# First expert stage of a four-layer kernel: three of sixteen token tiles dense instead of four, the first sorted group one tile larger, and several steps of VectorE, TensorE and GpSimd in other places

## The chip, the core and the metric

The program runs on one core of a Trainium2 chip. Its engines take instructions from queues of their own: TensorE (PE; its weight loads are listed as PEld), VectorE (DVE), ScalarE (ACT), GpSimd (POOL) and SyncE (SP), which here issues nearly all plain DMAs. They meet in semaphores only. The order of each engine's instructions is the order in which the program is written. The metric is the device time of one execution, in microseconds (us), as a median of runs.

## What is computed

Four layers with residual sums run over `x`, 4 batches x 512 positions x 128 features (2048 tokens of D = 128):

```python
x = x + ssm(layernorm(x), ...)          # linear recurrence over time, then W_out
x = x + ffn(layernorm(x), ...)          # first expert stage
x = x + attention(layernorm(x), ...)    # 16 heads of 64, relative bias, softmax
x = x + ffn(layernorm(x), ...)          # second expert stage, same weights

def ffn(x, router_w, w_gate, w_up, w_down):      # 8 experts, hidden 256
    xt = x.reshape(-1, D)
    logits = xt @ router_w.T
    topk_vals, topk_idx = jax.lax.top_k(logits, 2)
    g = jax.nn.sigmoid(topk_vals)
    g = g / (g.sum(axis=-1, keepdims=True) + 1e-10)
    out = jnp.zeros_like(xt)
    for e in range(8):
        ge = jnp.sum(jnp.where(topk_idx == e, g, 0), axis=-1)
        h = jax.nn.silu(xt @ w_gate[e]) * (xt @ w_up[e])
        out = out + ge[:, None] * (h @ w_down[e])
    return out.reshape(B, S, D)
```

Each token needs two of eight experts. Which two is known only when the logits of the layer are there.

## The kernel before

**Tiling.** The 2048 tokens are 16 tiles of 128, in four chunks of four tiles (QT = 4). `x_res` holds all of x on the chip. A product in fp32 precision is made of three products in a faster format (`three`, L301): high x high, high x low, low x high. So each operand exists as a rounded high part, made by ScalarE, and as a low part, the difference, made by VectorE or GpSimd.

**Two ways through an expert stage.** *Dense*: a set of tiles goes through all eight experts and the gates, zero where an expert was not chosen, weigh the sums. For expert e TensorE computes gates and up parts (`dense_gate_up`, 12 products with all tokens of the set as columns), ScalarE the silu, VectorE the product (`dense_products`), TensorE the tile sums (`dense_down`), and VectorE adds them to x with the gates as factors (`dense_add`). Nothing has to be sorted for it. *Sorted*: the tokens of a group of tiles are ordered by expert. VectorE works out the places (the `group_*` functions), GpSimd sends each tile's normalised rows to its two places in memory, one indirect DMA each (`scatter_rows`), SyncE loads the sorted rows back when all sends of the group have landed (`load_sorted`: blocks 0 to 3 as one transfer, the rest as another), and TensorE then takes them in blocks of 128 rows of one expert. A turn of sorted rows (`sorted_turn`) makes columns of rows, for up to four blocks at a time; such a piece has one bank for its outputs, a copy that empties it (`quad_out`), and one store to memory. For each block there follow three products of 512 columns (L303 to L305), the silu, the product, a turn, a copy and the down product (`block_down`). GpSimd gathers each tile's two rows back (`gather_rows`), and VectorE adds them to x with their gates (`combine`).

**The first expert stage before.** Chunk 0 (tiles 0 to 3) is dense. Group 0 is tiles 4 to 7: 8 sends, 15 blocks, in pieces of 4, 4, 4, 3. Group 1 is tiles 8 to 15: 16 sends, 23 blocks, in pieces of 4 five times, then 3. In all 38 blocks (`B1`). While the dense part runs, the norm of chunk 1 (`ln_*` with 1) and then the places of groups 0 and 1 are worked out on VectorE. GpSimd first makes low parts of weights: four experts, the query and key weights (L2079, 1024 columns each), the value weights (L2088), the other four experts. Then it sends, the sends of group 0 spaced over experts 4 to 7 and those of group 1 over expert 7 and the first blocks, one each time a step of TensorE is done. The norm that attention needs of chunk 0 is made in blocks 3 to 12 of the sorted part, right behind the dense sums, and its turn (`ln_turn`) stands on TensorE at block 11. The rows of group 0 come back from block 21 on and are added at blocks 31 and 32. Behind block 37 attention's first projections start (`enter`).

**The second expert stage** uses the same blocks in three groups: 2 (tiles 0 to 7, 23 blocks), 3 and 4 (four tiles, 15 blocks each). Group 4 is the last one; its routing is done between blocks of group 3, VectorE's and TensorE's parts in a hand-written order by steps of one block: the weights of group 3 at step 9, the sum and the maxima of group 4 at 11, its mask at 13, the gate weights of group 4 (`group_weights`) at 14, and at 15 the count (`group_count`, TensorE) and the places (`group_start`, VectorE). All waits are on constants.

## Time and profile before

| | |
|---|---|
| median of three runs (734.63, 734.91, 731.36) | 734.63 us |
| the profiled execution, its own time | 732.48 us |
| its span in the trace | 730.7 us |
| mean granted TensorE clock | 0.99 |
| TensorE busy | 688.5 us, 94% |
| VectorE busy | 550.6 us, 75% |
| ScalarE busy | 452.9 us, 62% |
| GpSimd busy | 306.4 us, 42% |
| chain that ended last | PE 77%, DVE 14%, ACT 4%, issue 3% |

Times within the program are counted from the start of the span. The dense part begins at about 49.7, the first block of the sorted part at 96.4, attention's first projection at 156.3. A row of a timeline gives the start, the duration of what stands in the row (of all of it, where it says x4 or so), the engine, the line and the operation, output first; in square brackets stands idle time of the engine ahead of it and what ended it. A row with x16 of an engine that works without a pause gives the cost of one as an average. A busy TensorE row can still be a slow one: the granted clock of a stretch is in the windows.

### The profile page before, as it was taken

The numbers are of one execution on the slowest core, as the hardware profiler recorded it, in microseconds if no ns is written. First come the engines' busy times: TensorE is split into PE (matmuls) and PEld (weight loads), VectorE is DVE, ScalarE is ACT, GpSimd is POOL, SyncE is SP. The second block draws the span as 40 slices with busy tenths as digits, with TensorE's granted clock in tenths as the row PEclk, the third lists the DMA queues.
The fourth block names the chain that finished last, engine by engine and source line by source line (L and its number), as shares of the span: only waits on it lengthen the run. The fifth ranks groups of instructions, "written<-read, shape, count | busy, mean of one in ns | idle before, by whom it ended". The sixth has DMA issues, their size and how long they took to land.

```text
span 730.7 us, 14144 instructions
## 1 busy us (share of the span) xinstructions
PE 688.5 (94%) x4316; PEld 485.0 (66%) x4316; DVE 550.6 (75%) x1712; ACT 452.9 (62%) x1097; POOL 306.4 (42%) x391
## 2 busy tenths in 40 slices
PE   4898998997899999998999999999999899998998
PEld 2576887885565755665666666576666566677886
DVE  7898774568998768877767769666988788476486
ACT  5546244556677757666757767667666768454554
POOL 1053471406674434333433333324365676503561
PEclk9999999999999999999999999999999999999999
DMA  9900054228000000000000000070003222032532
GB/s 236 290 5 0 30 202 137 71 68 304 19 23 4 3 0 1 2 1 1 1 1 1 2 1 1 1 190 3 1 9 105 73 69 62 23 92 66 133 84 59
DMA packets 52375, 43.37 MB, mean 59 GB/s; under 512 B 3296, under 2 KB 46944, under 8 KB 52304
## 3 DMA queue, kind: packets, MB, share of 16 engines
q1 hardware_dynamic: 48976, 35.63, 16.8%
q0 software_dynamic: 3328, 6.83, 3.2%
q8 instruction: 39, 0.64, 0.4%
q14 instruction: 32, 0.26, 0.1%
HBM read 26.70 MB, written 15.75 MB: 58 GB/s over the span
## 4 chain that ended last, share of the span: by engine, by line
PE 77%; DVE 14%; ACT 4%; issue 3%; POOL 0%; DMA 0%; DVEq 0%; ACTq 0%; POOLq 0%
PE psum L1166 15%; PE psum L1148 12%; PE psum L1133 12%; PE psum L303 8%; PE psum L305 6%; PE psum L304 6%; PE psum L816 5%; PE psum L1090 4%; DVE prob L1329 3%; PE psum L783 3%; PE psum L485 2%; ACT prob L1598 1%; PE psum L736 1%; DVE probT L1336 1%; DVE ln_stats L318 1%
## 5 line engine op out<-in xcount | busy, mean ns | idle before, releaser
L1745 POOL TENSOR_SCALAR prob<-prob,ones 128x512 f32<-128x512 f32 x256 | 174.6, 694 | 257.5 <-DVE ones L1315 257.0
L1598 ACT ACTIVATE prob<-prob,ones 128x512 f32<-128x512 f32 x256 | 183.5, 718 | 128.5 <-DVE ones L1329 128.5
L1329 DVE CUSTOM_DVE_ANT_0 prob<-psum,bias_band 128x512 f32<-128x512 f32 x256 | 161.6, 687 | 59.8 <-PE psum L1133 56.7
L1148 PE MATMUL psum<-ident,prob 128*128 128x128 f32 x1024 | 124.3, 273 | 2.0 <-DVE ones L1329 1.6
L1166 PE MATMUL psum<-probT,v 128*64 128x512 f32 x512 | 124.0, 605 | 0.0
L1148 PEld LDWEIGHTS psum<-ident,prob 128*128 128x128 f32 x1024 | 114.6, 141 | 12.5 <-issue 4.1
L1336 DVE COPY probT<-psum 128x512 f32<-128x512 f32 x128 | 82.2, 678 | 8.2 <-PE psum L1148 8.2
L1604 ACT COPY probT<-psum 128x512 f32<-128x512 f32 x128 | 74.0, 578 | 1.1 <-PE psum L1148 0.7
L832 DVE TENSOR_TENSOR hid_s<-silu_s,psum 128x256 f32<-128x256 f32 x91 | 38.0, 419 | 43.0 <-ACT silu_s L825 41.9
L825 ACT ACTIVATE silu_s<-psum 128x256 f32<-128x256 f32 x91 | 34.8, 384 | 56.7 <-PE psum L305 53.5
L1166 PEld LDWEIGHTS psum<-probT,v 128*64 128x64 f32 x512 | 31.0, 136 | 55.1 <-issue 54.2
L1133 PEld LDWEIGHTS psum<-qkT_hi 64*128 64x128 f32 x256 | 24.0, 184 | 54.1 <-issue 49.4
L1133 PE MATMUL psum<-qkT_hi 64*128 64x512 f32 x256 | 57.3, 444 | 0.9 <-ACT v L1615 0.6
L816 PE MATMUL psum<-ws_down,hT 128*128 x364 | 57.5, 281 | 0.0
L1133 PE MATMUL psum<-qkT_lo,qkT_hi 64*128 64x512 f32 x256 | 50.6, 391 | 0.0
L1133 PE MATMUL psum<-qkT_hi,qkT_lo 64*128 64x512 f32 x256 | 50.3, 389 | 0.0
L1343 DVE TENSOR_TENSOR qkT_lo<-psum,qkT_hi 128x512 fp32r<-128x512 f32 x64 | 44.0, 688 | 8.3 <-ACT qkT_hi L1593 8.1
L816 PEld LDWEIGHTS psum<-ws_down,hT 128*128 128x128 f32 x364 | 49.2, 196 | 1.1 <-issue 0.6
L1598 ACT ACTIVATION_READ_ACCUMULATOR prob<-prob,ones 128x1 f32 x256 | 48.2, 188 | 0.0
L303 PE MATMUL psum<-ws_hi,sortedT_hi 128*128 x91 | 43.2, 475 | 0.3 <-DVE hid_s L832 0.3
L727 POOL TENSOR_TENSOR ws_lo<-ws_raw,ws_hi 128x512 fp32r<-128x512 f32 x16 | 20.5, 1286 | 44.7 <-DVE bias_band L2158 34.1
L1593 ACT CAST qkT_hi<-psum 128x512 fp32r<-128x512 f32 x64 | 37.1, 580 | 2.4 <-PE psum L305 1.5
(308 smaller groups left out, 1256.4 us busy)
## 6 DMA issues: line engine op xcount, KB each, us to landing
bias_band<-bias_rows SPq DMA_DIRECT2D x16, 448.0 KB, 8.2
ys<-y SPq DMA_DIRECT2D x16, 256.0 KB, 2.3
ws_down<-in_w_down SPq DMA_DIRECT2D x4, 512.0 KB, 7.4
ws_raw<-in_w_gate SPq DMA_DIRECT2D x2, 768.0 KB, 6.3
ws_raw<-in_w_up SPq DMA_DIRECT2D x2, 768.0 KB, 8.1
xs<-zero SPq DMA_DIRECT2D x1, 1472.0 KB, 11.5
xs<-x_norm SPq DMA_DIRECT2D x1, 1472.0 KB, 6.8
sorted<-xs SPq DMA_DIRECT2D x2, 704.0 KB, 5.3
```

The costliest lines, as they stand in the source:

```text
L303: nc.tensor.matmul(dst, lh, rh, start=start, stop=False)
L304: nc.tensor.matmul(dst, lh, rl, start=False, stop=False)
L816: last = nc.tensor.matmul(bank[y_home(i)][:, j * P:(j + 1) * P], hT[stage_of(i)][:, i % 3, h * P:(h + 1) * P], ws_down[stage_of(i)][:, bas ...
L1133: last = nc.tensor.matmul(bank[scores_home(n) + h][:, :], lq[rows, 0, q], rk[rows, 1, :], start=(i == 0), stop=(i == 2))
L1148: last = nc.tensor.transpose(bank[turned_home(n) + h][:, j * P:(j + 1) * P], prob[:, n % PROBS, h, j * P:(j + 1) * P], ident[:, :])
L1166: last = nc.tensor.matmul(bank[PV_BANK][h * DK:(h + 1) * DK, :], v[:, kt, col], probT[:, u % 2, h, kt, :], start=(kt == 0), stop=(kt == QT ...
L1329: nc.vector.tensor_tensor_reduce(out=prob[:, buf, h, :], in0=bank[scores_home(n) + h][:, :], in1=row_bias, scale=-1.0, scalar=NEG_START, o ...
L1336: nc.vector.tensor_copy(probT[:, u % 2, 1, :, qt * P:(qt + 1) * P], bank[turned_home(n) + 1][:, :].rearrange("p (k q) -> p k q", k=QT)).th ...
L1343: nc.vector.tensor_tensor(qkl[u % 2][:, i, :], bank[home][:, :], qkh[u % 2][:, i, :].bitcast(F32), ALU.subtract).then_inc(a_pl, 1)
L1598: nc.scalar.activation(prob[:, buf, h, :], prob[:, buf, h, :], ACT.Exp, bias=peak[:, buf, h:h + 1], scale=-1.0, accum_out=total[:, buf, h: ...
L1604: nc.scalar.copy(probT[:, u % 2, 0, :, qt * P:(qt + 1) * P], bank[turned_home(n)][:, :].rearrange("p (k q) -> p k q", k=QT)).then_inc(a_ea, 1)
L1745: nc.gpsimd.tensor_scalar(prob[:, buf, h, :], prob[:, buf, h, :], inv[:, buf, h:h + 1], 1.0, ALU.mult, ALU.mult).then_inc(a_n, 1)
```

## The change

Its parts, in the order of the program:

- **Dense part.** Three tiles instead of four (`ND`, `D_TOK` 384 columns instead of 512, three sums per expert, smaller routing operations). Tile 3 goes to group 0, which now has five tiles, 10 sends and 17 blocks in pieces of 4, 4, 4, 3, 2 (`quad_sizes`). The stage has 40 blocks.
- **VectorE in the dense part.** The low part of the second two tiles of chunk 1 (`ln_low(1, 2, 4)`) stands ahead of the gates instead of behind them.
- **GpSimd.** The low parts of all eight experts are made in a row, then come the 10 + 16 sends, then the low parts of the value, query and key weights, then the 10 gathers. Sends 3 to 15 of group 1 wait for two blocks more each (`gu` i - 2 instead of i - 4), and sends 0 to 2 for later steps of the dense part.
- **The norm of chunk 0 for attention** moves from blocks 3 to 12 to blocks 28 to 37, since tile 3's rows are added only at block 27 (`combined(0, 0, 0)`). `ln_turn` moves from block 11 to block 36. The other combines of group 0 move from 31 and 32 to 38 and 39. `group_blocks(1)` moves from 12 to 13. `enter` and `quad_out` of the first piece of group 1 get a wait for the weights' low parts.
- **Buffers.** Several tiles lie elsewhere; the bank for the blocks' sums starts with the other parity, so that the first block's sum waits for all eight dense adds instead of seven. Groups 2 and 3 are loaded by one transfer each; `load_band(2)` waits for the first stores and combines.
- **Second expert stage.** The weights of group 3 are spread over steps 9 and 10, the count of group 4 is at step 14 instead of 15, and its places (`group_start`) are at 14, ahead of its weights, now at 15.

The diff, cut to its core:

```diff
-        GROUPS = [(QT, 2 * QT), (2 * QT, 4 * QT), (0, 2 * QT), (2 * QT, 3 * QT), (3 * QT, 4 * QT)]
+        ND = QT - 1
+        GROUPS = [(ND, 2 * QT), (2 * QT, 4 * QT), (0, 2 * QT), (2 * QT, 3 * QT), (3 * QT, 4 * QT)]
...
-        D_TOK = slice(0, BANK)
+        D_TOK = slice(0, ND * P)
...
-                    three(pe, bank[2 * half + w][:, :], ws_hi[0][:, col], ws_lo[0][:, col], xh[:, D_TOK],
+                    three(pe, bank[2 * half + w][:, D_TOK], ws_hi[0][:, col], ws_lo[0][:, col], xh[:, D_TOK],
                           xl[:, D_TOK]).then_inc(DN[name], 1)
...
-            for n in range(QT):
+            for n in range(ND):
                 for h in range(MT):
                     last = nc.tensor.matmul(bank[DY_BANK + e % 2][:, n * P:(n + 1) * P],
...
-        QUADS = [(g, b, min(4, nb - b)) for g, nb in enumerate(N_BLOCKS) for b in range(0, nb, 4)]
+        def quad_sizes(nb):
+            return [4] * (nb // 4 - 1) + [3, 2] if nb % 4 == 1 else [min(4, nb - b) for b in range(0, nb, 4)]
+
+        QUADS = [(g, sum(quad_sizes(nb)[:i]), n) for g, nb in enumerate(N_BLOCKS) for i, n in enumerate(quad_sizes(nb))]
...
         def gather_rows(pool, g, n, r):
             pool.wait_ge(GS["yd"][g], 16 * sum(quad[0] == g for quad in QUADS))
+            if g == 0:
+                pool.wait_ge(GS["gw"], 1)
+                pool.wait_ge(GS["bd"], 2)
...
-                return Y_BANK + q % 2
+                return Y_BANK + (LAST_QUAD0 - q) % 2
...
             if i == 0:
-                pe.wait_ge(DN["add"], E - 1)
-            if i == N_QUAD:
                 pe.wait_ge(DN["add"], E)
...
+            if q == QUADS_TO[0]:
+                dve.wait_ge(s_al, 3)
...
-                    if i == 12:
-                        pe.wait_ge(LN[2]["lo"], 1)
                     if j == 0 and 0 < q and q + 1 < Q1:
                         sorted_turn(pe, q + 1)
-                    if i == 11:
-                        pe.wait_ge(GS["xl"], q + 2)
+                    if i == 36:
+                        pe.wait_ge(GS["xl"], Q1)
                         ln_turn(pe, 2, 0, XT_BANK)
...
-                    if k in (7, 11, 15):
+                    if k in (7, 11, 14):
                         pe.wait_ge(GS["xl"], q + 2)
...
-                    if k == 15:
+                    if k == 14:
                         group_count(pe, LAST_G, XT_BANK)
...
-                if i == 3:
-                    dve.wait_ge(DN["add"], E)
-                    ln_stats(dve, 2, 0, 1)
...
-                if i == 12:
+                if i == 13:
                     group_blocks(dve, 1)
                 if i == 18:
                     group_weights(dve, 0)
+                if i == 28:
+                    dve.wait_ge(DN["add"], E)
+                    dve.wait_ge(GS["cb"], 2)
+                    ln_stats(dve, 2, 0, 1)
...
+                if i == 37:
+                    ln_low(dve, 2, 0, XT_BANK)
...
                 if i == 14:
+                    group_start(dve, LAST_G, XT_BANK)
+                if i == 15:
                     group_weights(dve, LAST_G)
-                if i == 15:
-                    group_start(dve, LAST_G, XT_BANK)
...
-            for i in range(2 * QT):
-                third_of_step(3 * 4 + 1 + i)
-                scatter_rows(pool, 0, i // 2, i % 2)
-            for i in range(4 * QT):
-                if i < 3:
-                    third_of_step(3 * 7 + i)
-                elif i < 5:
-                    pool.wait_ge(DN["dn"], i + 4)
-                else:
-                    pool.wait_ge(GS["gu"], i - 4)
-                scatter_rows(pool, 1, i // 2, i % 2)
-            for i in range(2 * QT):
-                pool.wait_ge(GS["gu"], 21 + i)
-                gather_rows(pool, 0, i // 2, i % 2)
+            def rows_out():
+                for i in range(2 * tiles_of(0)):
+                    third_of_step(3 * 4 + 1 + i)
+                    scatter_rows(pool, 0, i // 2, i % 2)
+                for i in range(4 * QT):
+                    if i == 0:
+                        third_of_step(3 * 7 + 2)
+                    elif i < 3:
+                        pool.wait_ge(DN["dn"], i + 6)
+                    else:
+                        pool.wait_ge(GS["gu"], i - 2)
+                    scatter_rows(pool, 1, i // 2, i % 2)
+
+            def rows_back():
+                for i in range(2 * tiles_of(0)):
+                    pool.wait_ge(GS["gu"], 24 + i)
+                    gather_rows(pool, 0, i // 2, i % 2)
...
-            qk_low(0)
-            qk_low(1)
-            pool.wait_ge(s_ah, 1)
-            nc.gpsimd.tensor_tensor(wvl[:, :], wv[:, :], wvh[:, :].bitcast(F32), ALU.subtract).then_inc(s_al, 1)
             for e in range(4, E):
                 split_low(pool, 0, e)
-            blocks_first_pool(pool)
+            rows_out, rows_back = blocks_first_pool(pool)
+            rows_out()
+            pool.wait_ge(s_ah, 1)
+            nc.gpsimd.tensor_tensor(wvl[:, :], wv[:, :], wvh[:, :].bitcast(F32), ALU.subtract).then_inc(s_al, 1)
+            qk_low(0)
+            qk_low(1)
+            rows_back()
...
             dense_products(dve, 2)
+            ln_low(dve, 1, 2, 4)
             dense_weights(dve)
             dense_pick(dve)
-            ln_low(dve, 1, 2, 4)
             dense_add(dve, 0)
```

**Place 1: VectorE around the dense gates.** L504 is the dense product (L509 after), L438 to L459 the gates chain (L443 to L464), L391 the low part of `xT` (L396), L512 the first `dense_add` (L517). Before:

```order
L443 TENSOR_SCALAR route_dense<-route_dense 128x4
L444 RECIPROCAL route_dense<-route_dense 128x4
L445 TENSOR_TENSOR route_dense<-route_dense 128x8
L452 TENSOR_TENSOR route_dense<-iota,route_dense 128x32 x2
L456 TENSOR_TENSOR route_dense<-route_dense 128x32 x2
L459 TENSOR_TENSOR route_dense<-route_dense 128x32
L391 TENSOR_TENSOR xT_lo<-psum,xT_hi 128x512
L512 SCALAR_TENSOR_TENSOR x_res<-psum,route_dense,x_res 128x128 x4
```

The same place after, from the products ahead of it:

```order
L509 TENSOR_TENSOR dense_hid<-dense_silu,psum 128x384 x2
L396 TENSOR_TENSOR xT_lo<-psum,xT_hi 128x512
L443 CAST route_dense<-route_dense 128x6
L445 TENSOR_SCALAR route_dense<-route_dense 128x6
L446 RECIPROCAL route_dense<-route_dense 128x6
L447 TENSOR_TENSOR route_dense<-route_dense 128x3
L448 TENSOR_SCALAR route_dense<-route_dense 128x3
L449 RECIPROCAL route_dense<-route_dense 128x3
L450 TENSOR_TENSOR route_dense<-route_dense 128x6
L457 TENSOR_TENSOR route_dense<-iota,route_dense 128x24 x2
L461 TENSOR_TENSOR route_dense<-route_dense 128x24 x2
L464 TENSOR_TENSOR route_dense<-route_dense 128x24
```

The low part has gone from behind the whole gates chain to ahead of it; the first `dense_add`, now of three tiles, follows the chain directly.

**Place 2: TensorE at the turns of group 1's first two pieces.** L736 (L747 after) is the turn of a piece; `grp_ld1` is the transfer of group 1's blocks 0 to 3, `grp_ld21` that of the rest; L816 (L825) is the second half of a block, L303 (L308) the start of the next. Before, with all waits:

```order
L736 MATMUL psum<-ident,sorted 128x128 [waits grp_xl,grp_ld1,ln2_lo]
L736 MATMUL psum<-ident,sorted 128x128 x3
L303 ISA [waits grp_mul,grp_xl]
...
L816 MATMUL psum<-ws_down,hT 128x128
L303 ISA [waits grp_mul,grp_xl]
...
L816 MATMUL psum<-ws_down,hT 128x128
L736 MATMUL psum<-ident,sorted 128x128 [waits grp_xl,grp_ld21]
```

After:

```order
L747 MATMUL psum<-ident,sorted 128x128 [waits grp_xl,grp_ld1]
L747 MATMUL psum<-ident,sorted 128x128 x3
L308 ISA [waits grp_mul,grp_xl]
...
L825 MATMUL psum<-ws_down,hT 128x128
L308 ISA [waits grp_mul,grp_xl]
...
L825 MATMUL psum<-ws_down,hT 128x128
L747 MATMUL psum<-ident,sorted 128x128 [waits grp_xl,grp_ld21]
```

Between the two turns there were the last blocks of group 0's piece of three, after the change those of its piece of two, since the turn of a piece stands at the first block of the piece before it.

**Place 3: VectorE in the last stage.** L832 (L841 after) is a block's product, L684 to L692 the gate weights of group 4 (L692 to L700), L644 to L650 its `group_start` (L652 to L658). Before:

```order
L832 TENSOR_TENSOR hid_s<-silu_s,psum 128x256 [waits grp_ht,grp_sg]
L684 TENSOR_SCALAR last_route<-last_route 128x8 [waits grp_ex]
L685 RECIPROCAL last_route<-last_route 128x8 [waits grp_rt]
...
L692 TENSOR_TENSOR last_route<-last_route 128x8 [waits grp_rt]
L832 TENSOR_TENSOR hid_s<-silu_s,psum 128x256 [waits grp_ht,grp_sg]
L854 COPY y<-psum 128x512 [waits grp_dn]
L644 TENSOR_SCALAR last_route<-psum 128x8 [waits grp_pm]
...
L650 SCALAR_TENSOR_TENSOR last_route<-last_route,psum 128x32 [waits grp_rt]
```

After:

```order
L841 TENSOR_TENSOR hid_s<-silu_s,psum 128x256 [waits grp_ht,grp_sg]
L652 TENSOR_SCALAR last_route<-psum 128x8 [waits grp_pm]
...
L658 SCALAR_TENSOR_TENSOR last_route<-last_route,psum 128x32 [waits grp_rt]
L841 TENSOR_TENSOR hid_s<-silu_s,psum 128x256 [waits grp_ht,grp_sg]
L865 COPY y<-psum 128x512 [waits grp_dn]
L692 TENSOR_SCALAR last_route<-last_route 128x8 [waits grp_ex]
L693 RECIPROCAL last_route<-last_route 128x8 [waits grp_rt]
...
L700 TENSOR_TENSOR last_route<-last_route 128x8 [waits grp_rt]
```

`group_start` stands where the weights stood, behind the next product, and the weights stand one product and one copy later.

## Rows read from the trace of the kernel before

**Rows 1.** TensorE's timeline in the sorted blocks: start us, us, engine, line, operation.

```profile
109.84 0.47 PE L303 MATMUL psum<-ws_hi,sortedT_hi 128*128 x1
...
111.21 0.48 PE L303 MATMUL psum<-ws_hi,sortedT_hi 128*128 x1
```

**Rows 2.** TensorE's timeline, dense products and one expert's tile sums.

```profile
50.44 0.40 PE L303 MATMUL psum<-xT_hi,ws_hi 128*128 128x512 f32 x1
...
50.67 0.39 PE L304 MATMUL psum<-xT_lo,ws_hi 128*128 128x512 f32 x1
...
55.25 1.95 PE L485 MATMUL psum<-ws_down,dense_hid 128*128 128x128 f32 x16
```

**Rows 3.** TensorE's gaps in the dense part; in brackets idle time before, releaser.

```profile
63.24 0.63 PE L376 MATMUL psum<-ident,x_norm 128*128 128x128 f32 x4 [1.27 <-ACT x_norm L369]
...
69.00 0.41 PE L633 MATMUL psum<-route_first,iota 128*128 128x40 f32 x2 [1.59 <-DVE xT_lo L391]
...
70.13 3.01 PE L485 MATMUL psum<-ws_down,dense_hid 128*128 128x128 f32 x16
```

**Rows 4.** Timelines: sends (POOL), loads (SPq), turns (PE); then tile sorted, landing.

```profile
88.26 0.95 POOL L706 DMA_INDIRECT xs<-x_norm,ones  x1 [0.30 <-issue]
...
111.06 0.95 POOL L706 DMA_INDIRECT xs<-x_norm,ones  x1 [0.41 <-PE psum L305]
...
90.58 0.36 SPq L1807 DMA_DIRECT2D sorted<-xs  x1
...
113.88 0.79 SPq L1808 DMA_DIRECT2D sorted<-xs  x1
...
94.00 0.60 PE L736 MATMUL psum<-ident,sorted 128*128 128x128 f32 x4
...
117.38 0.63 PE L736 MATMUL psum<-ident,sorted 128*128 128x128 f32 x4 [2.77 <-issue]
...
123.55 0.60 PE L736 MATMUL psum<-ident,sorted 128*128 128x128 f32 x4
...
DMA to landing us min/median/max: 3.0/4.7/8.8
```

**Rows 5.** Window of one microsecond: PE, PEld, DVE, ACT, POOL busy, PEclk, DMA share, GB/s.

```profile
119.00:120.00 1.00, 1.00 (x6) 1.00 (x5) 0.68 (x2) 0.42 (x2) 0.00 (x0) 0.50 1.05 297
```

**Rows 6.** Timelines of VectorE and TensorE in the last stage, and one window.

```profile
655.77 0.24 DVE L625 TENSOR_TENSOR_SCAN last_route<-over_hi,last_route 128x40 f32<-128x40 f32 x1
...
660.91 0.55 PE L736 MATMUL psum<-ident,sorted 128*128 128x128 f32 x3 [1.93 <-DVE last_route L650]
...
662.00:663.00 1.00, 1.00 (x5) 0.76 (x4) 0.56 (x1) 0.34 (x1) 0.00 (x0) 0.50 0.00 0
```

**Rows 7.** Timelines of VectorE and GpSimd around the dense gates.

```profile
61.25 0.17 DVE L349 SCALAR_TENSOR_TENSOR ln_shift<-ln_mean_var,ln_rstd 128x8 f32<-128x8 f32 x1
...
64.82 0.17 DVE L438 CAST route_dense<-route_dense 128x8 f32<-128x8 uint32 x1
...
66.60 1.40 DVE L456 TENSOR_TENSOR route_dense<-route_dense 128x32 f32<-128x32 f32 x2
...
68.26 0.69 DVE L391 TENSOR_TENSOR xT_lo<-psum,xT_hi 128x512 fp32r<-128x512 f32 x1
...
68.87 1.12 DVE L512 SCALAR_TENSOR_TENSOR x_res<-psum,route_dense,x_res 128x128 f32<-128x128 f32 x4
...
54.59 2.37 POOL L2088 TENSOR_TENSOR wv_lo<-wv_sb,wv_hi 128x1024 fp32r<-128x1024 f32 x1
...
66.67 1.28 POOL L727 TENSOR_TENSOR ws_lo<-ws_raw,ws_hi 128x512 fp32r<-128x512 f32 x1 [6.28 <-ACT ws_hi L722]
```

**Rows 8.** ScalarE's timeline, normalised rows, silus, high copy.

```profile
61.45 1.65 ACT L369 ACTIVATE x_norm<-x_res,ln_shift,ln_rstd 128x128 f32<-128x128 f32 x4 [2.45 <-DVE ln_shift L349]
...
63.01 1.05 ACT L496 ACTIVATE dense_silu<-psum 128x512 f32<-128x512 f32 x2
...
65.50 0.57 ACT L386 CAST xT_hi<-psum 128x512 fp32r<-128x512 f32 x1
```

111 lines of the change are left out of this document (62 added, 49 removed).

## The prediction

> **What bounds the kernel now.** I read the windows by stage first, then TensorE's timeline for gaps with what ended them, then the engine named there. In the sorted blocks TensorE goes without a pause: 1.37 us from one block's first product to the next [rows 1]. In the dense part it does not: 1.27 us go for normalised rows and 1.59 us for a low part, and the tile sums that start at 70.13 take 3.01 us for sixteen pieces that took 1.95 at 55.25 [rows 2, 3]. At 117.38 there is a gap of 2.77 us [rows 4], with a granted clock of 0.50 (1.2 GHz) in the microsecond at 119 [rows 5]. At the end of the kernel TensorE waits 1.93 us until 660.91, and 0.50 follows again at 662 [rows 6]. Each of the three slow stretches is about 3.4 us long in windows of one microsecond, so each gives up about 1.7 us. Everywhere else more work on TensorE is more time and less is less, as long as nothing else is late.
>
> **The dense stage, its work.** A product of 512 columns follows the last after 0.23 us [rows 2]; at 384 columns I take three quarters, so twelve save 12 x 0.058 = 0.7 us per expert. The tile sums save a quarter of 1.95, 0.5 [rows 2]. Eight experts: 9.5 us. Two more blocks cost 2 x 1.37 = 2.7 [rows 1], their turn of sorted rows 0.3. Net 6.5 us less work on TensorE. Whether that is time is decided by three waits.
>
> **First wait, the dense gates.** VectorE's four products before the norm are each some 0.15 us shorter (a quarter of 0.6), one part of GpSimd no longer falls into the norm, and one more index lies there: I put ln_shift at 60.1 where it ended at 61.4 [rows 7]. ScalarE then needs 1.65 for the rows, 0.95 for two silus (1.05 at 512 columns), 1.65 for the next rows and 0.57 for the high copy [rows 8]: 64.9. The low part, now first, ends at 65.6; before it began at 68.26 [rows 7]. So count and turn start 3.4 us earlier. But the gates chain, begun at 64.82 before [rows 7], now begins at 65.6, after VectorE stood idle. And it meets GpSimd. The two small operations of L456 took 1.40 us and ended as GpSimd's subtraction of 66.67 (1.28) ended [rows 7]: VectorE's two-input operation stood while GpSimd ran. The chain of 3.4 us up to 68.26 holds one such stand of 1.1, so it is 2.3 without. In the new order GpSimd's parts of experts 6 and 7 follow ScalarE's two high copies, at about 65.4 and 67.8, and both meet the chain: it ends near 70.3. Three adds at 0.28 (1.12 for four [rows 7]) follow, and dense_down(2) waits for them: 71.2 against 70.13, **+1.1 us**, after one gap of 4.6 us.
> The Trainium skill, page "SBUF — State Buffer", section "Who interferes with whom", has it that GpSimd and a VectorE instruction with two SBUF inputs contend, and that the second to issue waits for the whole of the other. By that rule the row agrees, and the moved low part buys a second stand. If there were no such rule, the sum would have 69.0 in place of 71.2 here.
>
> **Second wait, group 0's load.** From 71.2 TensorE is busy again, one slow stretch with it as before. Its work up to the third quarter of expert 7's gates: four gates and a three-quarter one, 2.1 x 3 + 1.5; four sums of 1.3; eight logits tiles, 1.7; a count, 0.4; slow, 1.7; a wait for a product, 0.3. In all 17.1 (estimates from rows 2): 88.3. The tenth and last send of group 0 waits for just this point and goes at 88.5; the eighth went at 88.26 [rows 4]. From that send to the load's issue were 2.32 us, from there to the turn of sorted rows at 94.00 another 3.42 [rows 4]. So the turn is at 94.2, **+0.2**. TensorE is there at 90.0 and waits 4.2 us, where it had no gap. A slow stretch came after each longer gap so far: **+1.7** (0.9 to 2.6, by how much of it lies in the gap itself). dense_down(7) gives 0.5 back, ln_turn has left this place (0.4). TensorE is then 1.1 late at block 12.
>
> **Third wait, group 1's load.** Its last send waits for the products of block 12 instead of block 10: 111.06 [rows 4] + 2 x 1.37 + 1.5 = 115.3, **+4.2**. The load is issued at 117.6, the turn of its first piece is at 121.6. TensorE comes to it three blocks later in its program than before, near 120.0: a gap of 1.6. But group 0 now ends with a piece of two blocks, so the turn of group 1's second piece, out of the other load, stands two blocks behind, not four. That load was issued at 113.88 and took 8.8 us [rows 4]; now 118.1 + 8.8 = 126.9, where TensorE would be ready at 124.9. Before, this turn was at 123.55 [rows 4]: **+3.35**. Behind it stand 22 blocks instead of 21 (+1.4), ln_turn (+0.4), a slow stretch that I take at 1.1 of 1.7, and a copy that now stands behind two combines (0.1). Attention starts **6.3 us** later (range 2 to 9).
>
> **What costs nothing, and its cover.** Group 0's rows are gathered from block 24 on, about 136, and combined at block 27, four us later; a landing over 4 us would show there. The norm at blocks 28 to 34 uses the slack that blocks 3 to 9 had. Low parts behind the sends run from 116.5 to 123.6 (2.37 us for 1024 columns [rows 7]); the copy that waits for them is at block 24, some ten blocks off. group_blocks(1) falls among them; if each of its operations waits for one, it is done at 123.6, under the cover of 126.9; without that cover it is 2 us. The first block's sum now waits for all eight adds, which stand a block ahead.
>
> **The end.** The count moves up a step, group_start ahead of the weights. The mask ends at 656.0 [rows 6], TensorE is there at 655.5: a wait of 0.55. group_start follows the next product and I have it done at 658.8; the turn that stood at 660.91 [rows 6] is due at 659.15. That is 1.75, and 1.7 for the slow stretch, since only a short gap is left: **-3.4 us**. Groups 2 and 3 are loaded long before use, so one load for two costs nothing. The sum is 6.3 - 3.4 = **+2.9 us**: 735.4 on the profiled 732.48, 737.5 on the median 734.63. The profiled run lies 2.2 below the median and one of the three lower still, so I take a value between, **736.3**.
>
> **Rivals.**
> A, the loads land early. The 8.8 us are a transfer beside others. If the second piece lands in 6.5, its wait of 2.0 is gone, with it the 1.1 of slow clock, and perhaps 1.7 more after 94: -0.2 to -1.9, **732 to 735**. For it: loads of this kind land in 3.0 to 8.8 [rows 4]. Against: the DMA share at 119 was 1.05 [rows 5], so the transfer was bound by itself.
> B, the work counts. The gates chain is not held twice, the sends move forward, the turns are not waited for: -6.5 - 3.4 = -9.9, less some 2.4 for waits that stay: **about 727**. For it: the work is really gone. Against: the last send of group 0 is tied to expert 7, and 5.7 us from send to turn don't shrink.
> C, slower: the end gives nothing. One step earlier TensorE also needs the result earlier. If group_start ends after 659.15, 0.35 us behind my estimate, a gap with its slow stretch can stay: +6.3, up to +8 with all slow stretches in full: **741**. For it: two table loads on ScalarE hold the product ahead of group_start. Against: the weights and a copy, 1.8 us, leave the way.
>
> **How the numbers follow.** Forecast 0.42, A 0.22, B 0.12, C 0.24. A measurement of this kernel can tell about 0.5%, 3.7 us, from no change. The forecast is +2.9 with 2.5 to each side, a third of it beyond 3.7: 0.14, with C 0.38 slower. B and the edges of A give 0.17 faster; 0.45 is left. The forecast's own range is 733 to 739. To leave out no more than 2 in 10 it takes in A and C up to its price: 730 to 741.
>
> **What would show it.** Right: the first turn of sorted rows within 0.5 of 94, after a gap of about 4 us and with 0.50 behind it; dense_down(2) near 71; two gaps between blocks 15 and 18; first scores 6 us later; no gap over 0.6 at the turn that was at 660.91. Wrong: that first turn before 92 (B), the second piece turned without a gap (A), a gap of 1.5 or more in the last stage (C).

## The result and the profile after

| | before | after |
|---|---|---|
| median of eight runs (range) | 732.09 us (731.08 to 734.99) | 739.73 us (736.09 to 741.96) |
| ratio, 95% interval | | 1.0089 (1.0060 to 1.0119) |
| profiled execution, own time / span | 732.48 / 730.7 us | 736.99 / 734.7 us |
| first product of the dense part | 49.66 | 48.87 |
| sum of expert 2 | 70.13 | 69.50 |
| turn of group 0's first piece | 94.00 | 92.83 |
| turn of group 1's first piece | 117.38 | 119.65 |
| turn of group 1's second piece | 123.55 | 127.43 |
| attention's first projection | 156.34 | 161.10 |
| turn of the last tiles' rows (L879, L890 after) | 642.49 | 649.06 |
| turn of group 3's last piece (three blocks) | 660.91 | 665.46 |
| third turn behind it | 678.73 | 682.35 |

The change makes the kernel slower by 0.9%, 6.5 us by the ratio, and the interval is clear of 1. The profiled execution of after is one of its quicker ones: its span is only 4.0 us longer. Stage by stage these 4.0 us are: start of the dense part -0.8, from there to attention's first projection +5.55, attention +1.8, from the turn of the last tiles' rows to the end of the span -2.6 (85.64 us instead of 88.21).

**The first stage.** TensorE's timeline of the changed kernel, the gaps and turns that answer to [rows 3] and [rows 4]:

```profile
61.12 0.63 PE L381 MATMUL psum<-ident,x_norm 128*128 128x128 f32 x4 [1.79 <-ACT x_norm L374]
...
69.50 2.18 PE L490 MATMUL psum<-ws_down,dense_hid 128*128 128x128 f32 x12 [3.88 <-DVE x_res L517]
...
92.83 0.63 PE L747 MATMUL psum<-ident,sorted 128*128 128x128 f32 x4 [3.61 <-DMA sorted<-xs]
...
119.65 0.66 PE L747 MATMUL psum<-ident,sorted 128*128 128x128 f32 x4 [0.76 <-DMA sorted<-xs]
...
123.97 0.41 PE L794 MATMUL psum<-ident,hid_s 128*128 128x128 f32 x2 [2.96 <-DVE hid_s L841]
...
127.43 1.04 PE L747 MATMUL psum<-ident,sorted 128*128 128x128 f32 x4
```

The dense work has shrunk, and its time has become waits. From expert 3's sums (76.30) to expert 6's (87.64) an expert took 3.8 us, before (from 78.08 to 92.22) 4.7. Yet from the first dense product to the turn of group 0's first piece 43.96 us pass instead of 44.34. The gaps of 3.88 and 3.61 us hold the rest. The gap of 2.96 is new and has VectorE as its releaser. The timelines of VectorE and GpSimd around both places:

```profile
64.56 1.07 DVE L445 TENSOR_SCALAR route_dense<-route_dense 128x6 f32<-128x6 f32 x1
...
67.01 1.22 DVE L461 TENSOR_TENSOR route_dense<-route_dense 128x24 f32<-128x24 f32 x2
...
116.14 6.08 DVE L680 TENSOR_TENSOR route_first<-route_first 128x184 f32<-128x184 f32 x1
...
64.33 1.27 POOL L738 TENSOR_TENSOR ws_lo<-ws_raw,ws_hi 128x512 fp32r<-128x512 f32 x1 [5.66 <-ACT ws_hi L733]
...
66.83 1.27 POOL L738 TENSOR_TENSOR ws_lo<-ws_raw,ws_hi 128x512 fp32r<-128x512 f32 x1 [1.23 <-ACT ws_hi L733]
...
114.98 2.38 POOL L2117 TENSOR_TENSOR wv_lo<-wv_sb,wv_hi 128x1024 fp32r<-128x1024 f32 x1
...
117.30 4.69 POOL L2106 TENSOR_TENSOR qk_lo<-qk_f,qk_hi 128x1024 fp32r<-128x1024 f32 x2
```

The comparison that is L680 here, in the kernel before:

```profile
114.84 0.34 DVE L672 TENSOR_TENSOR route_first<-route_first 128x184 f32<-128x184 f32 x1
```

An operation of 0.17 us (L445) takes 1.07 and ends as GpSimd's part ends (65.60). Two of 0.28 together take 1.22, again until 68.1. The comparison of `group_blocks(1)`, L680, begins at 116.14 among GpSimd's three subtractions and ends at 122.22, when the last of them has ended at 121.99.

**The clock.** Windows of one microsecond in the changed kernel, columns as in [rows 5]:

```profile
95.00:96.00 1.00, 1.00 (x7) 1.00 (x7) 0.00 (x0) 0.00 (x0) 0.00 (x0) 0.50 0.09 24
...
125.00:126.00 1.00, 1.00 (x3) 0.54 (x2) 0.00 (x0) 0.00 (x0) 0.00 (x0) 0.50 1.11 332
...
463.00:464.00 1.00, 1.00 (x5) 0.38 (x6) 0.29 (x1) 0.90 (x2) 0.77 (x2) 0.50 0.00 0
```

The granted clock is at 0.50 (1.2 GHz) behind the gaps of 3.61 and 2.96, as it is behind the one of 3.88 (in the microseconds at 71 and 72), and in this execution also in the midst of attention, behind a wait of 1.98 us.

**The end.** TensorE and VectorE in the last stage:

```profile
662.13 0.39 PE L641 MATMUL psum<-last_route,iota 128*128 128x40 f32 x2 [0.45 <-DVE last_route L633]
...
665.46 0.49 PE L747 MATMUL psum<-ident,sorted 128*128 128x128 f32 x3
...
682.35 0.60 PE L747 MATMUL psum<-ident,sorted 128*128 128x128 f32 x4
...
664.55 0.19 DVE L658 SCALAR_TENSOR_TENSOR last_route<-last_route,psum 128x32 f32<-128x32 f32 x1
```

The gap of 1.93 us of [rows 6] is gone, and the count waits 0.45 instead. From the turn of the last tiles' rows to the one at 682.35 pass 33.29 us, before (678.73) 36.24.

### The profile page after: what moved, and what is told of

It reads as the page before. It is cut to its first block, busy times and chain, and to the rows that moved or that the text cites. A ratio compares the mean times of both kernels' runs of the same rounds, so it can differ in the third digit from the quotient of the medians.

```text
span 734.7 us, 14173 instructions
## 1 busy us (share of the span) xinstructions
PE 686.8 (93%) x4304; PEld 483.0 (66%) x4304; DVE 554.0 (75%) x1710; ACT 453.2 (62%) x1102; POOL 311.0 (42%) x395
## 4 chain that ended last, share of the span: by engine, by line
PE 74%; DVE 13%; ACT 5%; issue 4%; DMA 2%; POOL 1%; SPq 0%; DVEq 0%; POOLq 0%; ACTq 0%
PE psum L1178 15%; PE psum L1160 12%; PE psum L1145 11%; PE psum L308 7%; PE psum L825 5%; PE psum L310 5%; PE psum L309 5%; PE psum L1102 4%; DVE prob L1340 3%; PE psum L794 3%; ACT x_norm L374 2%; ACT prob L1615 1%; PE psum L747 1%; DVE probT L1347 1%; DMA ssm_par<-in_ssm_par 1%
## 5 line engine op out<-in xcount | busy, mean ns | idle before, releaser
L1178 PE MATMUL psum<-probT,v 128*64 128x512 f32 x512 | 125.6, 612 | 0.0
L841 DVE TENSOR_TENSOR hid_s<-silu_s,psum 128x256 f32<-128x256 f32 x93 | 38.6, 418 | 39.9 <-ACT silu_s L834 38.7
L825 PE MATMUL psum<-ws_down,hT 128*128 x372 | 58.2, 279 | 0.0
L825 PEld LDWEIGHTS psum<-ws_down,hT 128*128 128x128 f32 x372 | 49.4, 193 | 1.2 <-issue 0.6
L1615 ACT ACTIVATION_READ_ACCUMULATOR prob<-prob,ones 128x1 f32 x256 | 48.3, 189 | 0.0
L308 PE MATMUL psum<-ws_hi,sortedT_hi 128*128 x93 | 44.1, 474 | 0.4 <-DVE hid_s L841 0.4
L794 PE MATMUL psum<-ident,hid_s 128*128 128x128 f32 x186 | 36.1, 276 | 3.1 <-DVE hid_s L841 3.0
## 6 DMA issues: line engine op xcount, KB each, us to landing
xs<-zero SPq DMA_DIRECT2D x1, 1472.0 KB, 11.1
```

Source lines behind the costliest of these rows:

```text
L308: nc.tensor.matmul(dst, lh, rh, start=start, stop=False)
L794: last = nc.tensor.transpose(bank[HT_BANK + i % 2][:, h * P:(h + 1) * P], s_hid[stage_of(i)][:, i % 4, h * P:(h + 1) * P], ident[:, :])
L825: last = nc.tensor.matmul(bank[y_home(i)][:, j * P:(j + 1) * P], hT[stage_of(i)][:, i % 3, h * P:(h + 1) * P], ws_down[stage_of(i)][:, bas ...
L1178: last = nc.tensor.matmul(bank[PV_BANK][h * DK:(h + 1) * DK, :], v[:, kt, col], probT[:, u % 2, h, kt, :], start=(kt == 0), stop=(kt == QT ...
L1615: nc.scalar.activation(prob[:, buf, h, :], prob[:, buf, h, :], ACT.Exp, bias=peak[:, buf, h:h + 1], scale=-1.0, accum_out=total[:, buf, h: ...
```

## The experiments

Each kernel was timed in turns with the kernel before on the same chip. The groups ran on different chips, on which the kernel before took 732 or 742 us, so ratios are compared, and traces only within a group or from a kernel's own milestones. The changed kernel itself was timed again only beside a_lowlate, a_lowlate_ld3 and a_poolbefore; a_gb12, a_g0free, a_free and b_tail share a second chip, a_lnback, a_notail and a_best a third, and a_three has a fourth. How much the chip matters: from first product to first projection the kernel before took 106.68 us in its first trace and, with an edit that lies behind this stretch, 112.18 in b_tail.

| kernel | this / before, us | ratio (95% interval) | mean granted clock, this / before |
|---|---|---|---|
| after_again | 739.71 / 732.52 | 1.0092 (1.0071 to 1.0114) | 0.985 / 0.990 |
| a_lowlate | 736.77 / 732.52 | 1.0056 (1.0037 to 1.0076) | 0.986 / 0.990 |
| a_lowlate_ld3 | 732.85 / 732.52 | 1.0007 (0.9990 to 1.0024) | 0.990 / 0.990 |
| a_poolbefore | 733.09 / 732.52 | 1.0018 (0.9999 to 1.0036) | 0.991 / 0.990 |
| a_gb12 | 747.44 / 742.22 | 1.0068 (1.0041 to 1.0096) | 0.984 / 0.991 |
| a_g0free | 746.90 / 742.22 | 1.0072 (1.0043 to 1.0100) | 0.983 / 0.991 |
| a_free | 757.54 / 742.22 | 1.0214 (1.0178 to 1.0250) | 0.977 / 0.991 |
| b_tail | 740.55 / 742.22 | 0.9969 (0.9939 to 0.9998) | 0.992 / 0.991 |
| a_lnback | 742.09 / 741.70 | 1.0027 (0.9998 to 1.0055) | 0.987 / 0.991 |
| a_notail | 747.33 / 741.70 | 1.0090 (1.0059 to 1.0122) | 0.984 / 0.991 |
| a_best | 740.60 / 741.70 | 0.9991 (0.9965 to 1.0017) | 0.988 / 0.991 |
| a_three | 740.50 / 741.46 | 1.0000 (0.9972 to 1.0028) | 0.988 / 0.991 |

The mean granted clock is the mean over a kernel's runs. 0.001 of it is 0.74 us of 735 given up.

**The changed kernel again.**

> The changed kernel unchanged, as the measure for the others of this group on the same chip. 1.006 to 1.012 times the kernel before, with the gaps of 3.9, 3.6 and 3.0 us that its first trace shows.

As expected. Its profiled execution (741.31) has the same gaps, and three slow stretches in attention where the first trace of after has one. Two of the three places in its TensorE timeline, and the windows behind all three:

```profile
193.71 0.50 PE L308 MATMUL psum<-wv_hi,xT_hi 128*128 128x512 f32 x1 [1.11 <-DVE v L1359]
...
466.83 0.66 PE L381 MATMUL psum<-ident,x_norm 128*128 128x128 f32 x4 [1.98 <-DVE x_norm L365]
...
196.00:197.00 1.00, 1.00 (x4) 0.24 (x2) 0.59 (x2) 0.03 (x1) 0.97 (x2) 0.50 0.00 0
352.00:353.00 1.00, 1.00 (x4) 0.00 (x0) 0.00 (x0) 0.00 (x0) 0.00 (x0) 0.50 0.00 0
468.00:469.00 1.00, 1.00 (x4) 0.24 (x2) 0.69 (x1) 0.61 (x2) 0.21 (x1) 0.50 0.00 0
```

The kernel before has the same two waits in its trace, and the clock stays at 1.00 behind them:

```profile
187.77 0.50 PE L303 MATMUL psum<-wv_hi,xT_hi 128*128 128x512 f32 x1 [1.10 <-DVE v L1348]
...
457.67 0.63 PE L376 MATMUL psum<-ident,x_norm 128*128 128x128 f32 x4 [1.98 <-DVE x_norm L360]
...
459.00:463.00 4.00, 4.00 (x26) 2.33 (x23) 2.55 (x8) 1.54 (x4) 0.05 (x1) 1.00 0.00 0
```

From first projection to the turn of the last tiles' rows attention took 486.15 us before, 487.96 with one such stretch and 490.83 with three: 1.6 to 1.8 us each. The other eleven traces, on all chips, fit this: 486.38 and 486.40 us without a stretch (a_poolbefore, a_lnback), 487.74 to 488.09 with one (a_best, a_free, a_gb12, b_tail), 489.41 and 489.56 with two (a_g0free, a_notail), 491.02 to 491.27 with three (a_lowlate_ld3, a_three, a_lowlate). So attention's length followed the number of its slow stretches.

**group_blocks(1) one block earlier.**

```diff
-                if i == 13:
+                if i == 12:
                     group_blocks(dve, 1)
```

> The changed kernel with one edit: group_blocks(1) on VectorE one block earlier, at 12 instead of 13. In the trace of the changed kernel its first operation, a comparison with two operands in SBUF, takes 6.08 us from 116.14 to 122.22, while GpSimd makes three low parts from 114.98 to 121.99, and TensorE then waits 2.96 us for a product. Theory V (VectorE stands while GpSimd runs): one block earlier it begins at about 114.5, ahead of GpSimd's 114.98, and takes 0.34; the gap of 2.96 is gone, and the turn of group 1's second piece comes at 124.6 (its load is issued at 116.81 and takes up to 7.8) or earlier instead of 127.43, so the kernel is 2.8 us faster, up to 4.7 with the slow stretch at 125 gone too. Theory L (the transfer is what ends last there, as the prediction had it): the turn stays within 0.5 us of 127, and the time within 0.5 us of the changed kernel.

Neither: nothing was gained, and the load was not what TensorE waited for. VectorE and GpSimd of this kernel, and TensorE behind them:

```profile
119.15 0.34 DVE L680 TENSOR_TENSOR route_first<-route_first 128x184 f32<-128x184 f32 x1
119.53 0.35 DVE L682 TENSOR_REDUCE route_first<-route_first 128x23 f32<-128x184 f32 x1
119.91 7.00 DVE L683 TENSOR_SCALAR ones<-route_first 128x23 int32<-128x23 f32 x1
...
119.92 2.38 POOL L2117 TENSOR_TENSOR wv_lo<-wv_sb,wv_hi 128x1024 fp32r<-128x1024 f32 x1
122.25 4.62 POOL L2106 TENSOR_TENSOR qk_lo<-qk_f,qk_hi 128x1024 fp32r<-128x1024 f32 x2
...
127.39 0.79 PE L308 MATMUL psum<-ws_hi,sortedT_hi 128*128 x1 [4.80 <-DVE sortedT_lo L761]
```

The comparison was through in time, but the third operation of the same step, with one operand in SBUF, met the start of GpSimd's run and stood for all of it. So the hold is no matter of two operands, and one block is not enough. The ratio, 1.0068, is not told apart from that of the changed kernel (1.0089 and 1.0092, on other chips).

**The low parts of the weights later.**

```diff
             rows_out()
+            pool.wait_ge(GS["bd"], 2)
+            pool.wait_ge(GS["gw"], 1)
             pool.wait_ge(s_ah, 1)
```

> The changed kernel with one edit: GpSimd's low parts of the value, query and key weights wait until VectorE has finished group_blocks(1) and group_weights(0), and so run at about 125 to 132, between the last send and the first gather at 136.7. One block earlier for group_blocks(1) was not enough: there its third operation, with one operand, took 7.00 us until GpSimd's low parts ended at 126.87. Theory V (VectorE stands while GpSimd subtracts, whatever the form): all three operations take under 0.4 us, the gap of 2.96 us (4.80 with the block earlier) ahead of the turn of group 1's second piece is gone. What is late next is that piece's load: issued at 116.8, 7.8 us to landing, 124.6, against a turn at 127.43 in the changed kernel: 2.8 us less, or 1.1 to 2.8 if a slow stretch stays. Theory L (the load lands last anyway): within 0.5 us of the changed kernel.

```profile
117.72 0.34 DVE L680 TENSOR_TENSOR route_first<-route_first 128x184 f32<-128x184 f32 x1
118.10 0.35 DVE L682 TENSOR_REDUCE route_first<-route_first 128x23 f32<-128x184 f32 x1
118.48 0.18 DVE L683 TENSOR_SCALAR ones<-route_first 128x23 int32<-128x23 f32 x1
...
124.48 0.41 PE L794 MATMUL psum<-ident,hid_s 128*128 128x128 f32 x2 [0.42 <-issue]
...
125.91 0.65 PE L747 MATMUL psum<-ident,sorted 128*128 128x128 f32 x4 [0.57 <-DMA sorted<-xs]
```

Theory V is shown: 0.34, 0.35 and 0.18 us, and where after_again has a gap of 3.18 there is one of 0.42. The medians differ by 2.9 us, by the ratios 2.6 (six runs each, 735.99 to 738.38 us against 738.25 to 741.31). The load is next: issued at 118.40, landed after 7.5 us, and TensorE waits 0.57 us for it. First product to first projection is 110.14 us, after_again 112.39, before 106.68.

**Group 1's rows in three transfers, on top of that.**

```diff
+                if g == 1:
+                    sp.dma_start(xs_in[g][:, 4:8, :], of_block[:, 4:8, :]).then_inc(GS["ld2"][g], 16)
+                    sp.dma_start(xs_in[g][:, 8:, :], of_block[:, 8:, :]).then_inc(GS["ld3"], 16)
+                    return
```

> The kernel with the late low parts, and group 1's rows loaded as three transfers (blocks 0 to 3, 4 to 7, 8 to 22) instead of two, so that the second piece waits for four blocks and not for nineteen. The first transfer of four blocks lands 2.8 to 3.4 us after its issue, the one of nineteen 7.8. If the late low parts leave TensorE waiting for the second load, the second piece's turn comes at about 121 to 122, when TensorE is there, and 1.5 to 2.8 us go, with a slow stretch of 1.7 perhaps. If theory L is wrong and TensorE is not waiting for the load there, within 0.5 us of the kernel with the late low parts.

The second piece's turn no longer waits:

```profile
125.18 0.60 PE L748 MATMUL psum<-ident,sorted 128*128 128x128 f32 x4
```

First product to projection is 108.95, 1.2 us less. The medians differ by 3.9. The rest is clock: the mean is higher by 0.0034, 2.5 us fewer given up. Nothing in the first stage explains that. Its profiled execution, the slowest of its twelve (737.10), has the three slow stretches of attention too.

**GpSimd in its order of before.**

```diff
+            qk_low(0)
+            qk_low(1)
+            pool.wait_ge(s_ah, 1)
+            nc.gpsimd.tensor_tensor(wvl[:, :], wv[:, :], wvh[:, :].bitcast(F32), ALU.subtract).then_inc(s_al, 1)
             for e in range(4, E):
                 split_low(pool, 0, e)
...
             rows_out()
-            pool.wait_ge(s_ah, 1)
-            nc.gpsimd.tensor_tensor(wvl[:, :], wv[:, :], wvh[:, :].bitcast(F32), ALU.subtract).then_inc(s_al, 1)
-            qk_low(0)
-            qk_low(1)
```

> The changed kernel with GpSimd's order of before: low parts of four experts, of the query, key and value weights, of the other four experts, then the sends. Theory V: the gap of 2.96 us goes as with the late low parts, since nothing of GpSimd meets group_blocks(1); but 7.1 us of subtractions come back ahead of the dense gates, between 50 and 57, where the norm of the second half of chunk 1 runs on VectorE, and put off what follows: the expert's low parts, the norm's last steps and with them the gates and the turn at 61.12 by 0 to 1 us. In sum 1 to 3 us less than the changed kernel. If the moved low parts were worth what they cost: 0 to 1 us more than the changed kernel.

```profile
56.68 1.22 DVE L340 SCALAR_TENSOR_TENSOR ln_newton<-ln_rstd 128x8 f32<-128x8 f32 x1
...
61.53 0.63 PE L381 MATMUL psum<-ident,x_norm 128*128 128x128 f32 x4 [3.00 <-ACT x_norm L374]
...
68.96 2.69 PE L490 MATMUL psum<-ws_down,dense_hid 128*128 128x128 f32 x12 [1.80 <-DVE x_res L517]
...
68.38 1.28 POOL L738 TENSOR_TENSOR ws_lo<-ws_raw,ws_hi 128x512 fp32r<-128x512 f32 x1 [2.37 <-ACT ws_hi L733]
```

The norm is held in two operations instead of one (L335, with one input, and L340), and TensorE waits 3.00 us for its rows instead of 1.8. In exchange expert 7's low part comes at 68.38, behind the gates chain, and the gap of 3.88 is 1.80. The two together are nearly the same as in the changed kernel: 20.89 us from the first product to this sum, against 20.63 to 20.65. What is won lies at group 1 (first product to projection 109.80 instead of 112.39) and in the clock, 0.991 against 0.985. The move of the low parts, then, bought 0.2 us ahead of the gates, and the kernel with it is slower by 5.4 us by the ratios (6.6 by the medians). Of that the trace accounts for 2.6 us in the first stage; the rest goes with the clock, and that the move lowers the clock is not shown.

**The low part behind the gates again.**

```diff
-            ln_low(dve, 1, 2, 4)
             dense_weights(dve)
             dense_pick(dve)
+            ln_low(dve, 1, 2, 4)
```

> The changed kernel with one edit undone: the low part of the second two tiles of chunk 1 stands behind the dense gates again, as before. In the changed kernel the gates chain begins at 65.40 behind the low part, VectorE stands in it twice (1.07 and 1.22 us for operations of some 0.16 and 0.28), each time until GpSimd's subtraction ends, and TensorE waits 3.88 us for the first dense add. Theory G (two stands because of the place): with the chain back at about 63.4, right behind the products, it meets GpSimd's part of 65.36 only, or that part and the one of 67.86 only at its end; the first add is done 1 to 2 us earlier, and dense_down(2) starts at 68.5 to 69.5 instead of 70.53. Whether that is time is decided at the turn of group 0's first piece, which waits for a load whose sends hang on TensorE's steps: 0 to 2 us less than the changed kernel. Rival: the low part comes 3 us later, the count and group 0's places with it, and the tenth send goes later: the turn at 94.1 moves back, 0 to 2 us more than the changed kernel.

```profile
64.67 1.26 DVE L464 TENSOR_TENSOR route_dense<-route_dense 128x24 f32<-128x24 f32 x1
...
64.63 1.26 POOL L738 TENSOR_TENSOR ws_lo<-ws_raw,ws_hi 128x512 fp32r<-128x512 f32 x1 [5.66 <-ACT ws_hi L733]
...
66.71 0.42 PE L641 MATMUL psum<-route_first,iota 128*128 128x48 f32 x2 [2.01 <-DVE xT_lo L396]
...
91.93 1.09 PE L747 MATMUL psum<-ident,sorted 128*128 128x128 f32 x4 [4.44 <-DMA sorted<-xs]
```

Theory G. The chain meets one part of GpSimd, in its last operation, and TensorE waits 2.01 us once. The sum starts at 67.65. The gain is not given back: first product to first turn of sorted rows is 42.76 us, in a_notail, which has the changed kernel's first stage on the same chip, 45.54, and to the first projection 113.82 against 117.27. The sends hang on TensorE's steps and move with them. How much of the ratio of 1.0027 is owed to this edit is open: the changed kernel was not timed on this chip, and a_notail (1.0090) also lacks the edit of the last stage.

**Sends without waits for TensorE's steps**, group 0's ten alone, and all 26.

```diff
-                    third_of_step(3 * 4 + 1 + i)
                     scatter_rows(pool, 0, i // 2, i % 2)
```

> The changed kernel, but GpSimd's ten sends of group 0 no longer wait for steps of TensorE, only for their places and rows. In the changed kernel the places are written at 72.07, the first send goes at 74.52, the third after 1.73 us of waiting at 78.69, the rest follow every 1.26 us, the tenth at 87.53, and TensorE waits 3.61 us for the turn of group 0's first piece at 92.83. Theory P (the spacing makes the gap): sends from 72.2 on every 1.26 to 1.47 us, the tenth at 83.6 to 85.5, the load 2 to 3.9 us earlier, the turn at 89.2 to 90.8; 2 to 3.6 us less, and up to 1.7 more if the slow stretch at 94 goes with the gap. Theory N (the sends cost VectorE or TensorE time where they are not spaced): the dense part between 72 and 89 grows by 1 us or more and gives the gain back, the time stays within 1 us of the changed kernel.

> The changed kernel with all 26 sends of the first stage without waits for steps of TensorE. Group 1's places are written at 86.4; sixteen sends of 1.26 us put the last at about 105.5 instead of 113.99, the load's issue at 108, the turn of group 1's first piece without a wait. Theory P: the gaps of 3.61 us at 92.83 and 0.76 at 119.65 are gone, and with the low parts now from 106.5 to 113.5 the comparison of group_blocks(1) (which moves forward with the blocks, to about 112) is held for at most 1.5 us instead of 5.7, so the gap of 2.96 is gone as well: 7 to 11 us less than the changed kernel. Theory N (unspaced sends cost as much elsewhere): within 2 us of the changed kernel.

For a_g0free the time is as theory N has it (1.0072), but not by the route it named. a_free fits neither: 1.0214, some 9 us slower than the changed kernel by the ratios, where N allowed 2. ScalarE in a_g0free, with GpSimd's last send of group 0; then ScalarE, GpSimd and TensorE in a_free, and a window of it:

```profile
87.86 0.87 ACT L501 ACTIVATE dense_silu<-psum 128x384 f32<-128x384 f32 x2 [11.29 <-remote]
...
85.04 0.99 POOL L714 DMA_INDIRECT xs<-x_norm,ones  x1 [0.30 <-issue]
```

```profile
86.16 0.87 ACT L501 ACTIVATE dense_silu<-psum 128x384 f32<-128x384 f32 x2 [11.09 <-remote]
...
113.97 0.38 ACT L834 ACTIVATE silu_s<-psum 128x256 f32<-128x256 f32 x1 [15.02 <-remote]
...
113.00 0.96 POOL L714 DMA_INDIRECT xs<-x_norm,ones  x1 [0.30 <-issue]
...
114.96 0.66 PE L794 MATMUL psum<-ident,hid_s 128*128 128x128 f32 x2 [12.14 <-issue]
...
104.00:108.00 4.00, 0.00 (x0) 0.00 (x0) 0.00 (x0) 0.00 (x0) 2.93 (x4) 0.62 0.14 49
```

In both, ScalarE stops with work at hand, at the third send of group 0, and goes on when that row of ten sends is over, 1.8 us behind its last one in either kernel. In a_free it stops again in group 1's row, from 98.95 on, and goes on 0.01 us behind the last of the sixteen. These waits have no engine as releaser. In the second of them all three compute engines are idle for 11 us while the DMA engines are at 0.14. In a_g0free the tenth send is indeed earlier (85.04), but the turn comes 48.3 us after the first product, where it came after 45.9 in a_gb12 on the same chip. So taking out the waits between the sends, which look like slack, stops the other engines. What ScalarE stands for is open. The traces list single packets of two instruction queues. One falls into the first stand of each kernel (in the microsecond at 85 of a_g0free and at 83 of a_free), 2 to 3 us before it ends, and one only at the very start of the second stand (99). That it stands for a late load of instructions is neither shown nor excluded.

**The edit of the last stage alone, on the kernel before; and the changed kernel without it.**

```diff
                 if i == 14:
-                    group_weights(dve, LAST_G)
-                if i == 15:
                     group_start(dve, LAST_G, XT_BANK)
+                if i == 15:
+                    group_weights(dve, LAST_G)
```

> The kernel before with the edit of the last stage alone: count and places of group 4 one step earlier and ahead of its weights, group 3's weights over two steps. Theory S (the sum of the prediction): the gap of 1.93 us at 660.91 and the slow stretch behind it are gone, 3.4 us less than the kernel before (2.9 to 3.9). Theory C (the places end too late still, or the wait only moves): a gap of 0.5 us or more stays with its slow stretch, 0 to 1.5 us less. In between, if the gap goes and the slow stretch comes at another place: 1.7 us less.

> The changed kernel with the last stage of before: count of group 4 at step 15, its places behind its weights, group 3's weights in one step. Theory S (the prediction's sum for the end): a gap of some 1.9 us before the turn of group 4's first piece and a slow stretch behind it come back: 2.9 to 3.9 us more than the changed kernel, a ratio of about 1.0135 to the kernel before. Theory C: less than 1.5 us more.

The mechanism is as theory S has it. In b_tail nothing stands before that turn, and the clock stays up behind it. (It is the turn of group 3's last piece; the two expectations name it as group 4's first.) Without the edit TensorE's timeline has the gap again, and a slow window behind it:

```profile
673.40 0.55 PE L747 MATMUL psum<-ident,sorted 128*128 128x128 f32 x3 [1.92 <-DVE last_route L658]
...
676.00:677.00 1.00, 1.00 (x3) 0.65 (x3) 0.00 (x0) 0.00 (x0) 0.00 (x0) 0.50 0.00 0
```

In time the kernel before gains 0.31% (0.02 to 0.61), 2.3 us, under the 2.9 to 3.9 of theory S, which the interval still reaches. The changed kernel without the edit does not bear S out: it stands at 1.0090 (1.0059 to 1.0122), below the 1.0135 of S, and with the edit at 1.0089 and 1.0092, on other chips. The gain is measured in the stretch from the turn of the last tiles' rows to the third turn behind group 3's last piece (33.29 us with the edit and 36.24 without it, in b_tail 33.84 and in a_notail 36.82), but in the whole time only on the kernel before, and there barely.

**Two combinations.** a_best is a_poolbefore with earlier sends and three transfers:

```diff
-                    third_of_step(3 * 4 + 1 + i)
+                    third_of_step(3 * 4 - 1 + i)
...
-                        pool.wait_ge(GS["gu"], i - 2)
+                        pool.wait_ge(GS["gu"], max(1, i - 3))
```

> The changed kernel with four edits: GpSimd's low parts in the order of before; each send of group 0 waits for a step two thirds of an expert part earlier (so that the pause falls behind the fourth send, not behind the second); the sends of group 1 wait for one block less (gu i - 3); group 1's rows in three transfers. The kernel with the first edit alone took 733.1 us with the first turn of sorted rows 3.66 us late at 92.37 and the turn of group 1's first piece 1.51 late at 119.84. Theory P: the tenth send goes 1.3 to 2.5 us earlier, the turn at 92.37 with it, and group 1's load 1.4 further: 2 to 4 us less than the kernel with the first edit, 729 to 731 us, a ratio of 0.995 to 0.998 to the kernel before. Theory N (the pauses between sends are needed by other engines): waits with no engine as their releaser appear on ScalarE or VectorE between 74 and 90, and the time is the same or more than with the first edit alone.

> The changed kernel with the three edits that each took a wait away: the low part behind the dense gates again (1.0027 times the kernel before by itself, where the changed kernel stood at 1.009), GpSimd's low parts of value, query and key weights behind group_blocks(1) and group_weights(0), and group 1's rows in three transfers (these two together 1.0007). Theory A (the three waits are separate and lie one behind the other on TensorE's path): the gaps of 3.88 us at the first dense add and of 3.18 behind group 1's first piece are 2.0 and under 0.8, the stretches add up, 1.0092 - 0.0065 - 0.0085 gives 0.994 (0.991 to 0.998). Theory B (the first one is given back: the turn of group 0's first piece waits for its load anyway, so what is saved ahead of it becomes a longer gap there): the gap at that turn grows by as much as the first one shrinks, and the ratio stays at 0.999 to 1.003.

a_best is 0.9991, above theory P's 0.995 to 0.998: the gap at the first turn is 2.79 us and the one at group 1's first turn is gone, but the interval holds 1. a_three is 1.0000, in the range of theory B. Its first gap is 1.99 and the one behind group 1's first piece is gone, but 5.02 us stand at the turn of group 0's first piece (3.61 to 4.46 in the kernels with the first gap at 3.9), so part of what is saved ahead of that turn is given back there, as B has it. In a_lnback, on another chip, it was not. The profiled execution of a_three has the three slow stretches in attention. No version is shown to beat the kernel before but b_tail, and that by an interval that ends at 0.9998.

## Why the prediction came out as it did

The direction was right, and the time, 739.7, lies in the range (730 to 741), but only by the part of it that was put there for rival C. The forecast's own range ended at 739, and the largest chance, 0.45, went to a change too small to be told. That the time lies in the range is luck in part. The size was wrong: +2.9 us was forecast, +6.5 measured. Step by step, times from the first dense product where the start had shifted (49.66 and 48.87):

- **Dense work.** 0.9 us less per expert where 1.2 was taken, so some 7 instead of 9.5. The twelve products gave 0.65 (forecast 0.7), the sums 0.2 to 0.45 (forecast 0.5), and a wait of 0.3 ahead of expert 6's sums took some back. The rest, that it turns into waits, was right: the turn of group 0's first piece moved by -0.4 (forecast +0.2), behind a gap of 3.61 (forecast 4.2), with 0.50 behind it.
- **First wait.** Two stands were forecast and two came. The sum of expert 2 is at 20.63 instead of 20.47: +0.2, not +1.1: the stands took 0.9 us each where I had 1.2 (the text says 1.1; 65.6 + 2.3 to "near 70.3" leaves 1.2), and the low part was done 0.4 earlier. a_lnback shows that the new place of the low part costs the second stand.
- **Second wait.** The tenth send went 38.7 us behind the first product, forecast 38.8, but by another chain: the sends run back to back from the third on (78.69, then every 1.26 us), so the tenth hangs on where the third starts and not, as I had it, on TensorE's work up to expert 7. That work was summed well: 17.3 us from expert 2's sums (69.50) to the third quarter of expert 7's gates (86.84), forecast 17.1. (The words there count one set of gates too many; the sum has three and a three-quarter one.) From that send to the turn were 5.3 us, not 5.7.
- **Third wait.** The last send at 113.99 (65.1 from the first product, before 61.4): +3.7 for +4.2. The turn of the first piece +3.1, of the second +4.7 where +3.35 was forecast, but not for the reason given. I had the load land at 126.9, 2.0 us late; it took 7.8 us and not 8.8, and in a_lowlate, where nothing else holds the turn, it is late by 0.57 us only. What made TensorE wait was a step put under "what costs nothing": `group_blocks(1)` among GpSimd's low parts. The hold itself was sized well (done at 123.6 at worst, it was done at 122.8). Wrong was its cover: I asked when its result is needed, and not what stands behind it on VectorE. The next product stands there, and TensorE needs that at 121. The price put on a hold without cover, 2 us, was right: without the hold the first projection comes 2.25 us earlier, and the kernel is 2.9 us faster by the medians. Of the +4.7 at the second turn, then, 2.25 is the hold, 0.9 the load (75.44 us from the first product in a_lowlate_ld3, 76.31 in a_lowlate), and 1.55 the later arrival of TensorE.
- **First projection.** +5.55, forecast 6.3. Here two errors cancel: less from the load, more from VectorE.
- **The end.** -2.95 up to the turn at 682.35, forecast -3.4 (up to the end of the span -2.6 are left), and rival C fell: `group_start` was done at 664.7, 0.7 us ahead of the turn.
- **What was left out.** Attention was taken as unchanged in length. It grew by 1.8 us in one trace and by 4.7 in the other, by slow stretches at waits that it had before. The mean clock of after_again is 0.985 against 0.990 before; with 0.9850 and 0.9897, time times one minus clock is 11.1 against 7.5 us. So half of the 7.2 us between their medians, 3.6, goes with the clock. The forecast had 1.1 us of it in sum: 1.7 and 1.1 more in the first stage, 1.7 less at the end. Attention is the largest single term of the miss, and whether the change brings its slow stretches about, or by what, is not shown.

Rival A was half right in its premise, the load takes less than 8.8 us, though not 6.5, and wrong in its result, since VectorE was later. Rival B fell: the turns are waited for. Rival C gave nearly the measured time for a cause that did not happen.

The Trainium skill, page "SBUF — State Buffer", section "Who interferes with whom", was quoted for two-input instructions alone. The same section also has `tensor_scalar` contend with GpSimd where it enters a two-port mode. Here such operations with one input stood too: 1.07 us for L445, 7.00 for L683 in a_gb12; which mode they ran in, no trace shows. By the section the one that issues first blocks the other for the whole instruction; here VectorE stood over three of GpSimd's in a row, 6.08 us where one of them takes 2.4, and did not get in between them. The measurement decides.
